# Attention scores of a hybrid transformer kernel: bf16 thirds on 32-column tiles, or fp32 on 32x32 tiles

## What is computed

```python
q, k, v = heads(X @ Wq.T), heads(X @ Wk.T), heads(X @ Wv.T)          # layer A
attn = softmax(where(causal, q @ k.T * 0.25, -inf)); x += (attn @ v) @ Wo.T
xk, xr = mix(x, x_prev, mu_k), mix(x, x_prev, mu_r)                   # feed-forward
x += sigmoid(xr @ Wr) * (square(relu(xk @ Wk)) @ Wv)
k = decayed_sum(heads(x @ Wk.T)); k = k / norm(k) * scale             # layer B
v = mix(v, v_next); v = v / norm(v) * scale
att = softmax(where(causal, k[1:] @ k.T, -inf)); x += (att @ v) @ Wc.T
```

## Time and profile before

| | |
|---|---|
| median of 3 runs | 3308.53 us |
| the profiled execution | 3312.66 us, its span 3310.9 us |
| mean granted TensorE clock | 0.944 of 2.4 GHz |
| TensorE matmul busy | 2950.6 us (89%), 42980 matmuls |
| ScalarE busy | 2226.6 us (67%) |
| VectorE busy | 1442.7 us (44%) |
| GpSimd busy | 830.9 us (25%) |
| DMA | 229841 packets, 225.66 MB |

### The profile page before, as it was taken

The page is one execution under the profiler, slowest core; times in us unless marked ns, Lnnn a source line. Parts: engine busy times, 40 slices in busy tenths (PEclk is TensorE's granted clock), DMA queues, the critical chain, the costliest instruction groups (busy, mean ns, idle before and its releaser), DMA issues.

```text
span 3310.9 us, 99622 instructions
## 1 busy us (share of the span) xinstructions
PE 2950.6 (89%) x42980; PEld 1307.6 (39%) x42980; DVE 1442.7 (44%) x3534; ACT 2226.6 (67%) x2487; POOL 830.9 (25%) x1278
## 2 busy tenths in 40 slices
PE   7799999999998799997998999998999988999887
PEld 3333343333434244443444444433333333333343
DVE  5232245545544652434333333444555545522444
ACT  2588876777776377673776677776777764777562
POOL 4122223233322222221222221322333321312111
PEclk9899999999999799997999999999999998999898
DMA  5222212222221123222222223221222221222111
GB/s 139 82 81 74 85 43 71 71 70 71 70 59 46 53 61 95 69 61 66 82 65 67 84 76 90 61 63 50 71 71 69 71 55 34 70 66 79 44 44 49
DMA packets 229841, 225.66 MB, mean 68 GB/s; under 512 B 33221, under 2 KB 212933, under 8 KB 229320
## 3 DMA queue, kind: packets, MB, share of 16 engines
q1 hardware_dynamic: 228504, 217.47, 23.0%
q10 hardware_dynamic: 816, 0.79, 0.1%
HBM read 146.80 MB, written 71.32 MB: 66 GB/s over the span
## 4 chain that ended last, share of the span: by engine, by line
PE 68%; DVE 17%; issue 8%; ACT 5%; POOL 1%; SPq 1%; DMA 1%; DVEq 0%; ACTq 0%; POOLq 0%
PE ps L857 42%; PE ps L1064 22%; ACT probs L813 4%; PE ps L869 3%; DVE pmax L1366 2%; DVE ln_st L1138 2%; DVE xn L1147 2%; DVE nw_u L1128 1%; DVE nw_u L1130 1%; DVE nw_y L1132 1%; DVE k_blk L1345 1%; DVE x_buf L1259 1%; DVE ln_mv L1141 1%; DVE o_blk L1408 1%; POOL probs L716 1%
## 5 line engine op out<-in xcount | busy, mean ns | idle before, releaser
L813 ACT ACTIVATE probs<-ps 128x1024 f32<-128x1024 f32 x2176 | 2078.0, 1093 | 714.5 <-PE ps L857 711.2
L857 PE MATMUL ps<-q_st,k_st 99*32 99x512 bf16 (+3 forms) x20480 | 1275.1, 353 | 43.2 <-issue 26.1
L1064 PE MATMUL ps<-probs,v_st 128*17 128x512 f32 (+3 forms) x10240 | 1201.0, 541 | 111.3 <-issue 76.5
L857 PEld LDWEIGHTS ps<-q_st,k_st 99*32 99x32 bf16 x20480 | 565.7, 97 | 850.8 <-issue 460.2
L716 POOL TENSOR_SCALAR_AFFINE_SELECT probs<-probs 128x256 f32<-128x256 f32 (+1 forms) x896 | 405.3, 468 | 1533.3 <-ACT probs L813 1526.5
L1064 PEld LDWEIGHTS ps<-probs,v_st 128*17 128x17 f32 x10240 | 288.7, 99 | 390.3 <-issue 169.5
L1408 DVE STREAM_TRANSPOSE o_blk<-ps 128x512 f32<-128x512 f32 x128 | 90.7, 709 | 449.6 <-PE ps L1064 447.7
L857 PE MATMUL ps<-xT,wT 128*32 128x512 f32 x2048 | 251.5, 609 | 1.8 <-issue 1.8
L869 PE MATMUL ps<-ident,xn 128*128 128x128 f32 x512 | 97.3, 323 | 117.6 <-DVE o_blk L1408 59.2
L1259 DVE TENSOR_TENSOR x_buf<-x_buf,ps 128x512 f32<-128x512 f32 x64 | 43.7, 683 | 316.9 <-PE ps L857 313.1
L640 POOL TENSOR_TENSOR parts<-rest,parts 128x512 bf16<-128x512 f32 x96 | 119.7, 1247 | 226.1 <-DVE parts L1170 226.1
(11 more groups left out here) (136 smaller groups left out, 2170.1 us busy)
## 6 DMA issues: line engine op xcount, KB each, us to landing
part_a<-parts SPq DMA_DIRECT2D x192, 128.0 KB
x_buf<-in_L_attn_a_X SPq DMA_DIRECT2D x32, 512.0 KB, 4.6
q_st<-part_a SPq DMA_DIRECT2D x128, 128.0 KB
o_chan<-o_out SPq DMA_DIRECT2D x64, 256.0 KB, 2.4
o_in<-o_chan SPq DMA_DIRECT2D x64, 256.0 KB, 4.5
q_st<-part_b SPq DMA_DIRECT2D x128, 128.0 KB
k_st<-part_a SPq DMA_DIRECT2D x64, 192.0 KB, 2.9
part_b<-parts SPq DMA_DIRECT2D x96, 128.0 KB
```

The lines of the kernel that those rows point to most:

```text
L813: nc.scalar.activation(probs[:, g % NP_BUF, :], ps[:, bk:bk + 2, :].rearrange("p a n -> p (a n)"), ACT.Exp, scale=SCALE[ATT[g // (NHG * NG ...
L857: last = pe.matmul(o[c:c + 32], kt[:, c:c + 32], q, **how)
L1064: last = pe.matmul(ps[32 * j:32 * j + VW, bank, q0:q0 + w], v_st[:, k % 2, kb, hg * HG + j, :], p, start=(kb == 0), stop=(kb >= TB * qc), ...
```

## The change

- Queries and keys stay fp32. Head `j` of an instance lies in partitions `32 j` to `32 j + 16`: 16 channels, and one row for the maximum (a row of zeros kept in HBM beside the queries; ones beside the keys). The thirds, `split` and `low_part` are gone; VectorE copies a unit from PSUM, GpSimd squares it for the bound, SyncE stores it once.
- A score matmul has 17 rows on a tile of 32 rows by 32 columns. The tiles of the two heads of a group are issued in turn (`zip` over the banks).
- The last group of a chunk becomes two groups of two heads with 256 columns in each bank: 72 slots per instance instead of 68, and `exp` of these reads 2 x 256 columns.
- The offsets of side parts are odd, so that they come in the slots that have value products, and further apart (`T_M` from 0..30 to 1..34, `T_B` from 34..71 to 41..68); `T_END` serves the last jobs.
- Row maxima are computed with 16 fp32 rows, and their negative is one fp32 row.

```diff
-MROW = DK * len(K_PART)
-KROWS = MROW + 3
+QROWS = DK + 1
...
-        groups.append([[(qc, d + 2, 2 * n, 2 * P, 2 * P, 0), (qc, d + 2, 2 * n + 1, 2 * P, 2 * P, 2 * P)]
-                       for n in range(2)])
+        for half in range(2):
+            groups.append([[(qc, d + 2, 2 * half + n, 2 * P, 2 * P, 0)] for n in range(2)])
...
-T_P = {"load": -10, "ln": 0, "t0": 7, "t1": 9, "u0": 11, ... "v1": 21, "n0": 24, "n1": 26, "flag": 29, "store": 4}
-T_M = {"load": -10, "o0": 0, "o1": 2, "t0": 9, "t1": 11, "diff": 11, "shift": 13, "k0": 16, "k1": 18, "r0": 20,
-       "r1": 22, "f0": 25, "f1": 27, "out": 30}
+T_P = {"load": -10, "ln": 0, "t0": 7, "t1": 9, "u0": 11, ... "v1": 21, "n0": 25, "n1": 27, "flag": 31, "store": 3}
+T_M = {"load": -10, "o0": 1, "o1": 3, "t0": 13, "t1": 15, "diff": 15, "shift": 17, "k0": 21, "k1": 23, "r0": 25,
+       "r1": 27, "f0": 29, "f1": 31, "out": 34}
...
-        k_st = sb("k_st", [P, HG, S], BF16)
-        q_st = sb("q_st", [P, HG, S], BF16)
+        k_st = sb("k_st", [P, S])
+        q_st = sb("q_st", [P, S])
...
+        def keys(j, rows=QROWS):
+            return k_st[32 * j:32 * j + rows, :]
...
-                for r, part, rows in K_RUNS:
-                    sp.dma_start(k_st[r * DK:(r + rows) * DK, :, c * CH:(c + 1) * CH], ...).then_inc(s_k[c], 16)
+                for j in range(HG):
+                    sp.dma_start(keys(j, DK)[:, c * CH:(c + 1) * CH],
+                                 src[0:DK, hg * HG + j, c * CH:(c + 1) * CH]).then_inc(s_k[c], 16)
...
-            sp.dma_start(rows_d, q_st[0:3, 0, :]).then_inc(s_rows, 16)
-            sp.wait_ge(s_rows, 16)
+            for i in range(2):
+                sp.dma_start(part_a[i, 0, DK], q_st[0:H, :]).then_inc(s_rows, 16)
+                sp.dma_start(part_b[i, DK, :, 1:S + 1], q_st[0:H, :]).then_inc(s_rows, 16)
+            sp.wait_ge(s_rows, 64)
...
-                for bank, units in enumerate(GROUPS[i]):
-                    o = ps[:, 2 * (g % NS_BUF) + bank, :]
-                    for qc, kb, j, q0, w, col in units:
+                for pair in zip(*GROUPS[i]):
+                    for bank, (qc, kb, j, q0, w, col) in enumerate(pair):
                         mask = masked and kb >= TB * qc
-                        last = matmul(o[:, col:col + w], k_st[0:KROWS, j, kb * P:(kb + 1) * P],
-                                      q_st[0:KROWS, j, qc * CH + q0:qc * CH + q0 + w], start=True, stop=not mask,
+                        last = matmul(ps[:, 2 * (g % NS_BUF) + bank, col:col + w], keys(j)[:, kb * P:(kb + 1) * P],
+                                      queries(j)[:, qc * CH + q0:qc * CH + q0 + w], start=True, stop=not mask,
                                       skip_group_check=mask)
...
-                    dve.wait_ge(s_high, 4 * j.at["p"] + i + 1)
-                    split(u, ps[:, part.bank, :], part)
+                    if u >= NPARTS:
+                        dve.wait_ge(s_store[u % NPARTS], stored(u - NPARTS))
+                    if u - NPARTS in SQUARED:
+                        dve.wait_ge(s_sq, SQUARED[u - NPARTS])
+                    copy_out(part, parts[:, u % NPARTS, :])
```

More of the change, by code:

```diff
@@ L132, in job_list @@
     for c in range(NCH):
-        jobs.append(Job("P", 1, c, 1, start(0, c) + FRONT - T_P["u2"]))
+        jobs.append(Job("P", 1, c, 1, start(0, c) + FRONT - 14))
     for k, b in ((1, 0), (2, 1), (5, 2), (6, 3)):
@@ L311, in hybrid_kernel @@
         row_max = sb("row_max", [P, NT])
-        m_part = [sb(f"m_part{i}", [NT, P], BF16) for i in range(3)]
-        m_rest = sb("m_rest", [NT, P])
+        m_neg = sb("m_neg", [NT, P])
         pf = probs[:, :, :].rearrange("p a n -> p (a n)")
@@ L376, in hybrid_kernel @@
         s_o_out = [sem(f"o_stored{i}") for i in range(2)]
-        s_mx = {n: sem("max_" + n) for n in ("scores", "used", "col", "turned", "step", "row", "placed")}
+        s_mx = {n: sem("max_" + n) for n in ("scores", "used", "col", "turned", "row", "placed")}
         block = ctx.enter_context(nc.Block())
@@ L649, in p_job @@
                 for i in range(4):
-                    yield j.t0 + T_P[f"u{i}"] + 2
-                    low_part(j.at["unit"] + i)
+                    yield j.t0 + j.off[f"u{i}"] + 2
+                    if i == 0:
+                        ffn = [o for o in JOBS if o.t0 < j.t0 and o.kind != "P"]
+                        if ffn:
+                            pool.wait_ge(s_part, ffn[-1].at["r1"].n + 1)
+                        if j.at["p"]:
+                            pool.wait_ge(s_part, [o for o in JOBS if o.t0 < j.t0 and o.kind == "P"][-1].at["n1"].n + 1)
+                    pool.wait_ge(*emptied(j.at[f"u{i}"]))
+                    unit = parts[:, (j.at["unit"] + i) % NPARTS, :]
+                    pool.tensor_tensor(squares[:, i, :], unit, unit, ALU.mult).then_inc(s_sq, 1)
             def m_job(j):
                 f = j.at["ffn"]
-                yield j.t0 + T_M["diff"]
+                yield j.t0 + j.off["diff"]
                 earlier = [i for i in JOBS if i.t0 < j.t0]
@@ L699, in m_job @@
                 last.then_inc(s_vb, 1)
-                for m in range(KT):
-                    yield j.t0 + T_B["low"] + 2 * m
-                    low_part(j.at["unit"] + m)
             def mask(g):
@@ L756, in p_job @@
                         nc.scalar.copy(xT[:, j.at["chan"] % 2, kt, :], ps[:, part.bank, :]).then_inc(s_side[part.bank], 1)
-                for i in range(4):
-                    yield j.t0 + T_P[f"u{i}"]
-                    u, part = j.at["unit"] + i, j.at[f"u{i}"]
-                    act.wait_ge(s_part, part.n + 1)
-                    if u >= NPARTS:
-                        act.wait_ge(s_store[u % NPARTS], stored(u - NPARTS))
-                    nc.scalar.copy(parts[:, u % NPARTS, 0, :], ps[:, part.bank, :]).then_inc(s_high, 1)
                 for i in range(2):
-                    yield j.t0 + T_P[f"v{i}"]
+                    yield j.t0 + j.off[f"v{i}"]
                     part = j.at[f"v{i}"]
@@ L1346, in m_job @@
                 settle()
-                yield j.t0 + T_B["split"]
-                for m in range(KT):
-                    step(nc.vector.transpose(kT[:, m, :], k_blk[:, m, :]))
-                settle()
+                yield j.t0 + j.off["split"]
                 for m in range(KT):
```

259 lines of the change are left out of this document (112 added, 147 removed).

## The result

| | before | after |
|---|---|---|
| median | 3310.93 us (3307.43 to 3314.87, 4 runs) | 3952.59 us (3948.38 to 3968.27, 4 runs) |
| ratio | | 1.195 (95% interval 1.191 to 1.198) |
| span of the profiled execution | 3310.9 us | 3946.7 us |
| mean granted TensorE clock | 0.944 | 0.933 |

The prediction was 3490 us, 3190 to 3720. The sign was right; the time lies 463 us above the forecast and outside the range.

The account below looks back on a forecast made before the run. ScalarE's exp bounds slots without side parts, TensorE those with them, plus stalls. Terms 24 + 36 + 6 + 11 + 116 - 12 = +181 us on 3312.66 gave 3494, or 3490 against the median; range 3190 to 3720.

Parts of the forecast that it names:

- Four heads run together: Scores: all four heads, 16 tiles, run together over two consecutive slots; 0.86 us per pair, against 3.44 if none overlap.
- rival B: Scores: the heads don't fully overlap; 4420 us, or 4890 if one column group holds back the next head; chance 0.18.
- Change of tile height: Each pair goes from 32x32 tiles to full-height tiles and back; 0.21 us per pair.
- rival A: Between scores and full-height tiles: changing tile height costs nothing; 3250 us; chance 0.24.
- Wide pairs: Slot pairs after the change: bare 2.05 us against 1.82, with projection 3.7 against 3.45, with transposes 2.6 against 2.3.
- Start and hole: Start: fewer store issues and low-part steps, -12 us; hole at the first transposes: ten slots cover VectorE's chain, 6.4 us out.
- the new narrow pair ... 1.25 us: New pair of 256 columns: 0.43 + 0.43 + 0.21 and waits, 1.25 us in place of one slot of 0.91.
- I take +16, the clock rising once the engine no longer pauses: Row maxima of flagged heads in fp32: TensorE becomes the bound, +9 to +38 us each, taken as +16, four times.
- Rival C: Maxima stay at 1.2 GHz, +22 us for each of 4, and tile-height changes cost 0.27; 3650 us; chance 0.10.
- What the masks cost: Flagged heads: mask matmuls separate the scores of a diagonal pair's two groups, with extra tile changes; +13 us each.
- Stalls: Ten slots instead of seven before the first transposes take 6.4 us out; 3 us per instance are left.

Follow-up runs that it names:

- streak: Matmuls alone, one form after another, no waits, not the kernel's computation; the whole took 1145 us in one run.
- the first run: Kernel before (bf16 thirds, 68 groups) with only the side parts of the feed-forward and layer B further apart; 3233.79 us, ratio 0.976 to the kernel before.

## Why the prediction was right, and where it was wrong

Two steps of the sum failed: the price of the pairs at the end of a chunk (about 240 of the 463 us), and the clock in the row maxima (118 us). The other parts of the mechanism held, with small sizes off; some 21 us in the last pair of instances stay unexplained.

- **Four heads run together** (rival B, 0.18). Right: the scores of a wide pair take 1.09 us for four heads, and the run with even side parts shows what it costs when they don't.
- **Change of tile height** (rival A, 0.24). Right, 0.25 us a round against 0.21. That the gap of the earlier trace rows belonged to height as well as width was the right choice.
- **Wide pairs.** Bare 2.07 in a streak and about 2.14 in the kernel against 2.05, projections 3.80 against 3.7, transposes 2.66 against 2.6. Small, but some 28 times an instance: with the branch, about 80 of the 463 us are left for them. The 2.05 was in part luck. Its 0.1 was for a wait for a buffer; in the streak nothing waits, and 0.10 is what starting twelve more tiles takes, of the 20480 further matmuls for which I had charged nothing.
- **Start and hole.** Right: -11.4 us, and no pause is left at the first transposes. The bf16 run with the wider spacing bears the reason out.
- **The step that failed: "the new narrow pair ... 1.25 us", and the diagonal pair taken as a bare one.** The sum had only one price for all pairs of 512 columns. The diagonal's two pieces were never worked out, though they double the matmuls per tile, and the narrow pair was paired with itself while the kernel pairs it with a wide one. Measured: 2.49 + 1.68 + 2.94 + 1.81 + 2.47 us where the sum had 9.45, so 1.9 at an end. Taken for all 4 x 32 ends, an estimate, that is about 240 of the 463 us. It fits the kernel without the branch, where an MA instance lasts 103.3 us: my 93.7 without stalls, 4 x 1.9, and 2.8 for wide pairs, projections and transposes make 104.1.
- **The step that was mis-sized: "I take +16, the clock rising once the engine no longer pauses".** The engine doesn't pause and the clock stays at 0.50; the pause grew by 49.5 us each instead of 16, 134 us too little in all. Rival C had the mechanism, but its 38 us a head (16 + 22) were short too: 58 us of stream were 64, and the pause ahead of them, 11.4 us in the earlier trace rows, is 16.6. What the masks cost was in order (13 us forecast, some 9 measured as 116.9 - 103.5 of an MA instance less 4 for the branch), which takes 16 off the 134.
- **Stalls.** I left 3 us an instance and 3.8 was measured, near by luck: not a wait that remained, but for the most part a new cost of the branch (23 us in 24 instances before, 91 after), a pause and the low clock behind it.
- **The range** had its upper end from rival C alone. Two mis-sized terms of the forecast itself could add, and I had not let them.

## What to carry to other kernels

Price each shape that a loop issues, not the commonest one: here the ends of chunks, with 16 of 72 groups, held about half of the error. Before pricing neighbours, write out the order in which the engine really gets them; running ahead by an odd number of groups pairs what the code never shows together. And when a bundle of changes loses, run its schedule alone: here a like spacing was worth 2.4% by itself.

## What the runs showed of the hardware

- A TensorE that was busy 100% had 0.50 of its clock with 16 of 128 rows at work in fp32 (750 to 890 us of the streaks), and 1.00 with 128 rows of fp32 or 99 of bf16 (925 to 1005, 1030 to 1110). The Trainium skill tells the clock by how busy the engine has been ("TensorE: Matmul & The Clock Gate", Part 1). The trace doesn't agree for the 16 rows: the engine was busy throughout, and the clock stayed at 0.50.
- VectorE's smallest steps can stand behind GpSimd. In the run with the values later, a step of 128x4 with two operands in SBUF, 0.16 us elsewhere, took 2.97 us, until 522.91, when GpSimd's second subtraction ended (522.89); a mask (L719) and the first subtraction lie within it too. Timeline of VectorE and GpSimd:

```profile
519.94 2.97 DVE L1133 SCALAR_TENSOR_TENSOR nw_u<-nw_u,nw_v 128x4 f32<-128x4 f32 x1
520.03 1.14 POOL L643 TENSOR_TENSOR parts<-rest,parts 128x512 bf16<-128x512 f32 x1
521.13 0.62 POOL L719 TENSOR_SCALAR_AFFINE_SELECT probs<-probs 128x512 f32<-128x512 f32 x1
...
521.74 1.15 POOL L643 TENSOR_TENSOR parts<-rest,parts 128x512 bf16<-128x512 f32 x1
```

  The Trainium skill has this as a lock on a shared port pair that makes the other engine wait in full ("SBUF — State Buffer", Who interferes with whom). The trace agrees that the wait is a full one. It is why later values made the next norm late: ahead of the first transposes this norm lasts 9.5 to 10.3 us in ten of the twelve ordinary MA instances, against 6.0 to 6.1 in the first run.
- Tiles of 32x32 start 7 ns apart behind a stretch of other tiles and 17 ns apart when 16 follow 16 at once; head by head or column by column makes no difference (2.07 us both).
